# A mixture-of-experts layer whose results are scattered to token order chunk by chunk, out of a ring of eight places

## The chip, the cores and the metric

The kernel runs on one core of one Trainium2 chip. The metric is the device time of one execution in microseconds (us). All data is fp32 unless said otherwise. A core has TensorE (PE), VectorE (DVE), ScalarE (ACT), GpSimd (POOL) and SyncE (SP), which issue instructions each in its own order and meet at semaphores, and 16 DMA engines that serve the queues of SP, ACT and POOL side by side.

## What is computed

There are 2 x 1024 = 2048 tokens of 256 numbers. The first half is cross attention to 77 context rows with a residual; the second half, which holds the change, is a feed-forward layer with a shared part and 32 experts of which every token takes one:

```python
    x = x + attention(layernorm(x), ctx, ...)
    h = layernorm(x)
    shared_out = (silu(h @ shared_gate) * (h @ shared_up)) @ shared_down     # 256 -> 512 -> 256
    logits = h @ gate_w                                                      # 32 experts
    e = argmax(logits);  xs = h * sigmoid(max(logits))
    routed_out[token] = (silu(xs @ gate[e]) * (xs @ up[e])) @ down[e]        # 256 -> 512 -> 256
    out = x + shared_out + routed_out
```

## The kernel before, in words

The 2048 tokens are 16 tiles of 128 (NT = 16), handled in 8 pairs (NU = 8). Five stages follow each other.

1. Attention, second norm and gate logits of the pairs (0 to 83 us in the profile), with seven of the sixteen units of the shared part between them. One unit (`shared_up`, line 951) is 128 of the 512 inner features for 512 tokens: 8 matmuls of 512 columns on PE, a Tanh on ACT (`shared_tanh`, 745), two DVE operations (`shared_h`, 526). `shared_down` (965) is the down projection of a pair, `shared_residual` (534) adds it to x1 on DVE.
2. Routing on DVE (lines 578 to 627): the rank of each token among the tokens of its expert, the number of chunks of each expert (a chunk is up to 32 tokens of one expert, LW = 32), `slot_i`, which is 32 times a token's chunk plus its place in it, `begin`, the column in the sorted order at which each chunk starts, `chunk_end` and `turn`, tables that PE and SP read, and `block_n`, the count of groups of 16 chunks. GpSimd scatters the scaled tokens to DRAM sorted by expert, 16 indirect DMAs of 128 rows of 1 KB (line 439). Units 7 to 11 of the shared part run beside it.
3. The sorted rows are loaded back (line 353), turned on PE (1017) and copied by ACT to `xsT` (780). PE then runs unit 12 of the shared part and begins the chunks.
4. The chunk loop (130 to 256 us): 79 chunks with these inputs. For chunk c the token columns are copied from `xsT` to `x_c`, half k = 0 as soon as PE has last used it (`x0_used`) and half k = 1 after `u_done`; GpSimd does both (453 to 458), after loading the chunk's column from `begin` to a register. PE does `gate_up` (1035, matmuls at 1039), ACT takes the Silu (`silu`, 784), DVE multiplies (`gated`, 641) and turns (`turn_h`, 649), PE does `down_of` (1052, matmuls at 1061), ACT copies PSUM to SBUF (`take_y`, 789), and DVE adds the two halves of the inner features (`sum_y`, 653). PE's order is gate_up(c+1), then down_of(c). The weights of an expert are 1.5 MB. They lie in a ring of 6 places; SP fills a place again for expert e + 6 once PE has done the last chunk of expert e (`refill`, 356), so 26 experts are loaded during the loop. The results of all chunks stay in SBUF (`y_halves`, 96 chunks, in the memory named `late`). ACT stores them to `slot_rows` in DRAM in chunk order, 16 chunks in two DMAs of 256 KB (`store_y`, 794): six of these are issued in the loop, the last four after it.
5. The end: when all stores have landed (line 460), GpSimd gathers the rows of each tile by `slot_i`, 16 indirect DMAs of 128 rows (463). PE runs units 13, 14 and 15 of the shared part (1118 to 1121) and the last two down projections (1122, 1123); DVE adds the gathered rows to x1 pair by pair (682), for the last two pairs after `shared_residual`; SP writes each pair to the output (371).

What sets the order: each engine's program is written out by hand and runs in order. SP has the loads, the refills, then the outputs. GpSimd has the scatter, then the x copies, then the gathers. DVE runs `shared_h(12)`, the chunk loop, `shared_h(13..15)`, then the sums. `zeros` is written to the unused part of `slot_rows` early (344), and GpSimd clears the rest of `late` (448).

## Time and profile before

| | |
|---|---|
| median of 3 runs | 292.94 us (292.06 to 293.19) |
| the profiled execution: device time | 291.1 us |
| its span, first to last instruction | 289.2 us |
| PE busy in the span | 250.5 us (87%) |
| DVE / ACT / POOL busy | 163.1 / 94.0 / 87.9 us |
| chunks | 79 |
| chunk loop (first gate_up to the end of the last down_of) | 130.0 to 255.6 us |
| bytes moved by DMA | 68.69 MB |

The span starts at the first instruction and all times in the rows are us from there. "PEld" is PE's weight load, a name with a q at its end (SPq, POOLq) is an engine's sequencer. "idle before" and the arrow tell how long an engine stood idle and what released it; "issue" is idle time that no wait in the profile explains. Matmul records overlap, so PE's busy time is not its work at full rate. The queue q0 is GpSimd's, q1 is SP's, q10 is ACT's.

### The profile page before, as it was taken

The numbers are of one execution on the slowest core, as the hardware profiler recorded it, in microseconds if no ns is written. First come the engines' busy times: TensorE is split into PE (matmuls) and PEld (weight loads), VectorE is DVE, ScalarE is ACT, GpSimd is POOL, SyncE is SP. The second block draws the span as 40 slices with busy tenths as digits, with TensorE's granted clock in tenths as the row PEclk, the third lists the DMA queues.
The fourth block names the chain that finished last, engine by engine and source line by source line (L and its number), as shares of the span: only waits on it lengthen the run. The fifth ranks groups of instructions, "written<-read, shape, count | busy, mean of one in ns | idle before, by whom it ended". The sixth has DMA issues, their size and how long they took to land.

```text
span 289.2 us, 12925 instructions
## 1 busy us (share of the span) xinstructions
PE 250.5 (87%) x4627; PEld 184.6 (64%) x4629; DVE 163.1 (56%) x490; ACT 94.0 (33%) x284; POOL 87.9 (30%) x248
## 2 busy tenths in 40 slices
PE   4997899997799899998979999999999999698800
PEld 3765666553375358856867888788788787543700
DVE  0655796878469543016656667666666667424333
ACT  2344875454230110235323333334333333211000
POOL 1262221111005777102222223222222222103772
PEclk9996899999999999999999999999999999999985
DMA  6999994000001325401998869999999999733565
GB/s 196 328 394 410 404 401 157 2 2 1 2 0 37 109 96 165 160 16 50 329 390 286 300 236 331 358 410 415 416 410 411 415 412 409 312 83 94 174 214 164
DMA packets 32559, 68.69 MB, mean 238 GB/s; under 512 B 3966, under 2 KB 18715, under 8 KB 32539
## 3 DMA queue, kind: packets, MB, share of 16 engines
q1 hardware_dynamic: 25723, 61.60, 56.4%
q0 software_dynamic: 1536, 4.20, 4.7%
q10 hardware_dynamic: 5280, 2.62, 3.5%
q8 instruction: 13, 0.21, 0.3%
q14 instruction: 7, 0.06, 0.1%
HBM read 59.49 MB, written 8.91 MB: 237 GB/s over the span
## 4 chain that ended last, share of the span: by engine, by line
PE 66%; DMA 9%; DVE 8%; issue 5%; POOL 5%; ACT 3%; POOLq 1%; SPq 1%; ACTq 1%; DVEq 0%
PE bank L1039 23%; PE bank L961 14%; PE bank L1061 11%; DMA ring_gu<-n_L_ffn_routed_up_w_dram 5%; PE bank L973 5%; POOL xs_flat L463 5%; PE bank L874 3%; PE bank L926 2%; PE bank L909 2%; DMA slot_rows<-late 2%; DVE h_place L531 1%; ACT h_place L749 1%; DVE h_place L532 1%; DMA h_place<-in_L_xattn_kernel_q_dram 1%; DMA xs_flat<-slot_rows,slot_i 1%
## 5 line engine op out<-in xcount | busy, mean ns | idle before, releaser
L1039 PE MATMUL bank<-ring_gu,x_c 128*32 128x128 f32 x2528 | 86.8, 275 | 6.6 <-issue 2.6
L1039 PEld LDWEIGHTS bank<-ring_gu,x_c 128*32 128x32 f32 x2528 | 64.8, 109 | 20.3 <-issue 8.1
L1061 PE MATMUL bank<-ring_d,h_place 128*32 128x128 f32 x1264 | 51.8, 274 | 2.3 <-issue 1.6
L646 DVE TENSOR_TENSOR h_place<-h_place,bank 128x128 f32<-128x128 f32 x79 | 31.2, 395 | 33.2 <-PE bank L1039 30.9
L456 POOL COPY x_c<-xs_flat 128x32 f32 x79 | 16.6, 210 | 101.2 <-PE bank L1039 88.5
L1061 PEld LDWEIGHTS bank<-ring_d,h_place 128*32 128x32 f32 x1264 | 36.1, 109 | 7.7 <-DVE h_place L651 5.3
L792 ACT COPY late<-bank 128x128 f32 (+1 forms) x79 | 21.0, 266 | 57.5 <-PE bank L1061 57.5
L973 PE MATMUL bank<-shd,h_place 128*128 128x256 f32 x128 | 28.4, 380 | 2.1 <-DVE h_place L532 2.1
L651 DVE STREAM_TRANSPOSE h_place<-h_place 128x128 f32<-128x128 f32 x79 | 24.6, 311 | 9.9 <-PE bank L1061 1.7
L787 ACT ACTIVATE h_place<-bank 128x128 f32<-128x128 f32 x79 | 21.9, 277 | 23.6 <-PE bank L1039 19.3
L531 DVE SCALAR_TENSOR_TENSOR h_place<-h_place,bank 128x512 f32<-128x512 f32 x16 | 11.0, 686 | 32.5 <-ACT h_place L749 32.5
L973 PEld LDWEIGHTS bank<-shd,h_place 128*128 128x128 f32 x128 | 24.2, 190 | 6.6 <-DVE h_place L532 3.0
L961 PE MATMUL bank<-late,shg 128*128 128x512 f32 x48 | 23.1, 603 | 4.3 <-DVE h_place L532 4.2
L749 ACT ACTIVATE h_place<-bank 128x512 f32<-128x512 f32 x16 | 9.6, 597 | 51.9 <-PE bank L961 51.9
L658 DVE TENSOR_TENSOR late<-late x79 | 22.4, 283 | 3.2 <-ACT late L792 0.7
L961 PE MATMUL bank<-late,shu 128*128 128x512 f32 x48 | 22.6, 593 | 0.0
L463 POOL DMA_INDIRECT xs_flat<-slot_rows,slot_i x16 | 15.2, 950 | 16.2 <-DMA slot_rows<-late 11.7
L439 POOL DMA_INDIRECT sorted_rows<-xs_flat,pos x16 | 16.1, 1006 | 11.1 <-DVE pos L596 6.5
L458 POOL COPY x_c<-xs_flat 128x32 f32 x79 | 16.6, 210 | 1.3
L961 PEld LDWEIGHTS bank<-late,shg 128*128 128x128 f32 x48 | 8.5, 190 | 12.9 <-issue 7.2
L961 PEld LDWEIGHTS bank<-late,shu 128*128 128x128 f32 x48 | 9.1, 190 | 11.5 <-issue 11.5
L538 DVE TENSOR_TENSOR x<-bank,x 128x512 f32<-128x512 f32 x8 | 5.4, 684 | 12.2 <-PE bank L973 12.2
(132 smaller groups left out, 261.9 us busy)
## 6 DMA issues: line engine op xcount, KB each, us to landing
ring_gu<-L_ffn_routed_gate_w_dram SPq DMA_DIRECT2D x32, 512.0 KB, 9.4
ring_gu<-n_L_ffn_routed_up_w_dram SPq DMA_DIRECT2D x32, 512.0 KB, 10.3
ring_d<-L_ffn_routed_down_w_dram SPq DMA_DIRECT2D x32, 512.0 KB, 10.3
slot_rows<-late ACTq DMA_DIRECT2D x10, 256.0 KB, 6.5
x<-in_x_dram SPq DMA_DIRECT2D x4, 512.0 KB, 7.3
slot_rows<-zeros SPq DMA_DIRECT2D x1, 2048.0 KB, 20.4
late<-sorted_rows SPq DMA_DIRECT2D x8, 256.0 KB, 3.4
out_dram<-x SPq DMA_DIRECT2D x8, 256.0 KB, 2.4
```

The costliest lines, as they stand in the source:

```text
L456: g_.tensor_copy(x_c[:, 0], xsT[:, 0, bass.ds(col, LW)]).then_inc(x0_part, 1)
L458: g_.tensor_copy(x_c[:, 1], xsT[:, 1, bass.ds(col, LW)]).then_inc(x1_part, 1)
L463: g_.indirect_dma_start(out=y_t[:, i, :], out_offset=None, in_=slot_rows, in_offset=bass.IndirectOffsetOnAxis(ap=slot_i[:, i:i + 1], axis= ...
L646: v.tensor_tensor(h_r.rearrange("p (m f) -> p m f", m=KF), g_silu.rearrange(rows, m=KF), bank[1][:, 0:P].rearrange(rows, m=KF), ALU.mult). ...
L651: v.transpose(hT, h_r).then_inc(hT_ready, 1)
L658: v.tensor_tensor(sums, other, sums, ALU.add).then_inc(y_ready, 1)
L787: a_.activation(g_silu, bank[0][:, 0:P], ACT.Silu).then_inc(silu_done, 1)
L792: a_.copy(y_halves[:, bass.ds(c, 1)].rearrange("p c d -> p (c d)"), bank[2][:, 0:DH]).then_inc(y_taken, 1)
L961: ins = te.matmul(dst[:], w[:, k, m * P:(m + 1) * P], xnT_of(g)[:, k], start=(k == 0), stop=(k == KD - 1))
L973: ins = te.matmul(bank[4 + w % 2][:, j * D:(j + 1) * D], h_s[:, w // 2 % 2, m, c:c + P], shd[:, m], start=(m == 0), stop=(m == KF - 1))
L1039: ins = te.matmul(bank[g][q * LW:(q + 1) * LW, 0:P], x_c[:, k], ring_gu[:, s, g, k, q * P:(q + 1) * P], start=(k == 0), stop=(k == KD - 1))
L1061: ins = te.matmul(bank[2][r:r + LW, 0:DH], hT[:, f * LW:(f + 1) * LW], ring_d[:, s, f, a * DH:(a + 1) * DH], start=(m == 0), stop=(m == HA ...
```

## The change

Each chunk's result now goes to DRAM by itself, in token order, in rows of half a token (512 B): GpSimd issues one indirect DMA of 64 rows for each chunk (rounded up to groups of eight chunks: 80 scatters for 79 chunks) to the table `y_rows`. Padding rows go to spare rows behind the table. The results lie in a ring of eight places, `y_ring`. `take_y` waits for its place to be free (`y_free`); GpSimd frees the place of chunk k - 2 (LAG = 2) after it has issued the scatter of chunk k and waited for that of k - 2 to land. After the last has landed, SP loads the table in order, 8 plain DMAs of 256 KB (1 KB rows, contiguous for a token), and then issues the outputs.

GpSimd no longer copies token columns: ACT does, between `silu` and `take_y`, after loading the chunk's column to a register. ACT's stores, the zeros, GpSimd's clear of `late` and the 16 gathers are gone. The row numbers are new work: four small functions on DVE between units 7 to 10 of the shared part make one-hot tables in bf16, PE multiplies them (16 matmuls of 64 weight columns and 104 columns, before unit 12), and DVE turns the product into row numbers. `groups_n` (three DVE instructions) takes the place of `block_n` (two). At the end DVE adds the loaded rows for all eight pairs first and the last two shared residuals after that; SP waits for both.

```diff
 GpSimd
-            with pool.Fori(0, n_chunks) as c:
-                col = pool.value_load(begin[0:1, bass.ds(c, 1)], min_val=0, max_val=T)
-                pool.wait_ge(x0_used, c + FREE1)
-                g_.tensor_copy(x_c[:, 0], xsT[:, 0, bass.ds(col, LW)]).then_inc(x0_part, 1)
-                pool.wait_ge(u_done, c + FREE1)
-                g_.tensor_copy(x_c[:, 1], xsT[:, 1, bass.ds(col, LW)]).then_inc(x1_part, 1)
-            pool.wait_ge(y_stored, HALVES * 16 * (blocks + 1))
-            pool.sem_inc(pool_waited, 1)
-            for i in range(NT):
-                g_.indirect_dma_start(
-                    out=y_t[:, i, :], out_offset=None, in_=slot_rows,
-                    in_offset=bass.IndirectOffsetOnAxis(ap=slot_i[:, i:i + 1], axis=0)).then_inc(y_in[i // 2], 16)
+            def next_rows(c, k):
+                g_.tensor_copy(rows_now[:, k:k + HALF_RING], rows_all[:, bass.ds(c, HALF_RING)]).then_inc(row_copied, 1)
+            def store_group(b, first=False):
+                for k in range(Y_RING):
+                    pool.wait_ge(row_copied, 2 * b + 1 + k // HALF_RING)
+                    pool.wait_ge(y_ready, Y_RING * b + k + 1)
+                    pool.sem_inc(y_sent, 1)
+                    g_.indirect_dma_start(
+                        out=y_rows, out_offset=bass.IndirectOffsetOnAxis(ap=rows_now[:, k:k + 1], axis=0),
+                        in_=y_ring[0:HR, k, :], in_offset=None).then_inc(y_out[k], 16)
+                    gone = (k - LAG) % Y_RING
+                    if k >= LAG:
+                        pool.wait_ge(y_out[gone], 16 * b + 16)
+                        pool.sem_inc(y_free, 1)
...
+                    if k == LAG:
+                        next_rows(Y_RING * b + HALF_RING, HALF_RING)
+                    if k == LAG + HALF_RING:
+                        next_rows(Y_RING * b + Y_RING, 0)
+            next_rows(0, 0)
+            store_group(0, first=True)
+            with pool.Fori(1, groups) as b:
+                store_group(b)
+            for k in range(Y_RING - LAG, Y_RING):
+                pool.wait_ge(y_out[k], 16 * groups)
+            pool.sem_inc(y_landed, 1)
 SyncE, behind the refills
+            sp.wait_ge(y_landed, 1)
+            for u in range(NU):
+                sp.dma_start(y_t[:, 2 * u:2 * u + 2], y_by_token[:, 2 * u:2 * u + 2]).then_inc(y_in[u], 16)
             for u in range(NU):
                 sp.wait_ge(sum_ready, u + 1)
+                if u >= NU - 2:
+                    sp.wait_ge(residual_ready, u + 1)
                 sp.dma_start(out_t[:, 2 * u:2 * u + 2], x1[:, 2 * u:2 * u + 2]).then_inc(out_done, 16)
 ScalarE
-            def take_y(c):
+            def take_y(c, place_c):
                 act.wait_ge(down_done, c + 1)
-                a_.copy(y_halves[:, bass.ds(c, 1)].rearrange("p c d -> p (c d)"), bank[2][:, 0:DH]).then_inc(y_taken, 1)
+                act.wait_ge(y_free, c + 1)
+                a_.copy(y_ring[:, place_c].rearrange("p c d -> p (c d)"), bank[2][:, 0:DH]).then_inc(y_taken, 1)
+            def take_x(c, col):
+                act.wait_ge(x0_used, c + FREE1)
+                a_.copy(x_c[:, 0], xsT[:, 0, bass.ds(col, LW)]).then_inc(x0_part, 1)
+                act.wait_ge(u_done, c + FREE1)
+                a_.copy(x_c[:, 1], xsT[:, 1, bass.ds(col, LW)]).then_inc(x1_part, 1)
+            def chunk(c):
+                col = column(c + 1)
+                silu(c)
+                take_x(c + 1, col)
...
             shared_tanh(3 * KF)
+            act.wait_ge(begin_ready, 1)
+            act.wait_ge(xsT_ready, NU + 1)
+            take_x(0, 0)
+            chunk(0)
+            with act.Fori(0, groups) as b:
+                for k in range(Y_RING):
+                    chunk(Y_RING * b + k + 1)
+                    take_y(Y_RING * b + k, slice(k, k + 1))
 VectorE, the end
+            for u in range(NU):
+                dve.wait_ge(y_in[u], 16)
+                rows = x1[:, 2 * u:2 * u + 2]
+                v.tensor_tensor(rows, rows, y_t[:, 2 * u:2 * u + 2], ALU.add).then_inc(sum_ready, 1)
+            for u in range(NU - 2, NU):
+                dve.wait_ge(sum_ready, NU)
+                shared_residual(u)
 TensorE, before unit 12 of the shared part
+            pe.wait_ge(hot_ready, 3)
+            for i in range(NT):
+                ins = te.matmul(bank[3][0:2 * LW, 0:SLOTS], hot_t[:, i].rearrange("p a t -> p (a t)"), hot_c[:, i],
+                                start=(i == 0), stop=(i == NT - 1))
+            ins.then_inc(found_done, 1)
```

## Rows read from the trace of the kernel before

**Rows 1.** Busy time by stretch (core 0: us, busy and count by engine, PEclk, DMA share, GB/s)

```profile
190.00:252.00 62.00, 58.48 (x1920) 49.59 (x1913) 39.44 (x120) 21.72 (x80) 16.36 (x79) 1.00 1.02 407
252.00:289.20 37.20, 20.35 (x140) 12.38 (x131) 13.38 (x24) 2.87 (x7) 15.62 (x18) 0.88 0.50 142
```

**Rows 2.** The chain of work that ended last (start us, us, what)

```profile
235.93 15.02 DMA ring_gu<-n_L_ffn_routed_up_w_dram
...
258.14 5.12 DMA slot_rows<-late
...
282.98 2.82 DMA xs_flat<-slot_rows,slot_i
```

**Rows 3.** The page's costliest groups: the gathers (busy us, mean ns, idle before)

```profile
L463 POOL DMA_INDIRECT xs_flat<-slot_rows,slot_i x16 | 15.2, 950 | 16.2 <-DMA slot_rows<-late 11.7
```

**Rows 4.** Timeline after the chunk loop (start us, us, engine line op, idle before)

```profile
255.55 1.99 PE L961 MATMUL bank<-xnT_last,shg 128*128 128x512 f32 x4
...
267.50 0.69 DVE L532 SCALAR_TENSOR_TENSOR h_place<-h_place,bank 128x512 f32<-128x512 f32 x1
...
268.24 7.17 PE L973 MATMUL bank<-shd,h_place 128*128 128x256 f32 x32 [2.13 <-DVE h_place L532]
...
285.90 0.69 DVE L682 TENSOR_TENSOR x<-x,xs_flat 128x512 f32<-128x512 f32 x1 [1.06 <-DMA xs_flat<-slot_rows,slot_i]
```

**Rows 5.** DMA issues by line (KB each, median us from issue to landing)

```profile
late<-sorted_rows SPq DMA_DIRECT2D x8, 256.0 KB, 3.4
```

**Rows 6.** GpSimd's scatter of stage 2, line 439, and one piece of its timeline

```profile
L439 POOL DMA_INDIRECT sorted_rows<-xs_flat,pos x16: 956/960/1437, 89.7 to 109.4; - x16
DMA to landing us min/median/max: 2.4/2.4/3.2
91.17 1.44 POOL L439 DMA_INDIRECT sorted_rows<-xs_flat,pos  x1 [0.30 <-issue]
```

**Rows 7.** Timeline of the chunk loop, one chunk

```profile
201.47 0.21 POOL L458 COPY x_c<-xs_flat 128x32 f32 x1
...
201.56 1.08 PE L1039 MATMUL bank<-ring_gu,x_c 128*32 128x128 f32 x32
201.86 0.27 ACT L792 COPY late<-bank 128x128 f32 x1 [0.68 <-PE bank L1061]
...
202.26 0.28 ACT L787 ACTIVATE h_place<-bank 128x128 f32<-128x128 f32 x1
202.35 0.28 DVE L658 TENSOR_TENSOR late<-late  x1
```

**Rows 8.** A table load to a register on PE's sequencer, line 1069

```profile
L1069 PEldq TENSOR_LOAD <-turn x32: 283/288/317, 130.3 to 251.3; - x32
```

**Rows 9.** Groups of instructions of ACT, shapes apart: the smallest copy-like one

```profile
L729 ACT ACTIVATE half_tanh<-top 128x2 f32<-128x2 f32 x8 | 1.5, 191 | 0.0
```

**Rows 10.** Timeline of the routing on DVE

```profile
93.78 0.14 DVE L624 TENSOR_SCALAR block_n<-block_n 1x1 int32<-1x1 int32 x1
```

**Rows 11.** The chain again: sixteen small matmuls in stage 1

```profile
53.19 0.69 PE bank L909 x16
```

**Rows 12.** Timeline at the start of the chunk loop

```profile
130.10 0.60 ACT L749 ACTIVATE h_place<-bank 128x512 f32<-128x512 f32 x1 [2.85 <-PE bank L961]
...
130.74 1.28 ACT L787 ACT_TABLE_LOAD   x1
...
132.04 0.28 ACT L787 ACTIVATE h_place<-bank 128x128 f32<-128x128 f32 x1
```

**Rows 13.** DMA queues and issues from 190 to 250 us (packets, MB, share of 16 engines)

```profile
q10 hardware_dynamic: 2112, 1.05, 5.8%
...
slot_rows<-late ACTq DMA_DIRECT2D x3, 256.0 KB, 9.5
```

**Rows 14.** DMA queues from 88 to 112 us, the scatter of stage 2

```profile
q0 software_dynamic: 768, 2.10, 24.4%
```

**Rows 15.** Waits from 140 to 255 us: PE's weight loads behind the x copies

```profile
PEld bank L1039 <- POOL x_c L456: 3.1, 8, 0.7
```

More of the change, by code:

```diff
@@ L289, in build_cross_attention_moe @@
         FREE2 = 2
+        LAG = 2
+        HALF_RING = Y_RING // 2
         EARLY_PARTS = {t: t - 7 for t in range(7, NU + 6)}
@@ new lines, in next_rows @@
+            def next_rows(c, k):
[12 more added lines that the diff above has]
+                        pool.sem_inc(y_free, 1)
+                    elif not first:
+                        pool.wait_ge(y_out[gone], 16 * b)
+                        pool.sem_inc(y_free, 1)
+                    if k == LAG:
+                        next_rows(Y_RING * b + HALF_RING, HALF_RING)
+                    if k == LAG + HALF_RING:
+                        next_rows(Y_RING * b + Y_RING, 0)
@@ new lines, in column @@
+            def column(c):
+                return nc.values_load(begin[0:1, bass.ds(c, 1)], engines=(mybir.EngineType.Activation,), min_val=0, max_val=T,
+                                      skip_runtime_bounds_check_because="held to the number of tokens where it is written")
+            def take_x(c, col):
[3 more added lines that the diff above has]
+                a_.copy(x_c[:, 1], xsT[:, 1, bass.ds(col, LW)]).then_inc(x1_part, 1)
@@ L826, in _ @@
+            with act.Fori(Y_RING * groups + 1, n_chunks) as c:
+                chunk(c)
+                take_y(c - 1, place_of(c - 1))
+            take_y(n_chunks - 1, place_of(n_chunks - 1))
             for n in range(3 * KF + 1, 4 * KF):
@@ L831, in _ @@
             te = nc.tensor
+            pe.sem_inc(y_free, Y_RING)
             for credit in (y_taken, y_taken, silu_done, h_ready, hT_ready, x0_used, u_done):
```

139 lines of the change are left out of this document (77 added, 62 removed).

## The prediction

> **What bounds the kernel now.** I read the busy time by stretch first. From 190 to 252 us PE is busy 58.5 of 62 us at full clock, and the DMA engines are full as well (share 1.02, 407 GB/s); ACT's 80 instructions are two for each chunk, so 40 chunks take 62 us, 1.55 us each. From 252 us on the picture is another one: PE is busy 20 of 37 us, DMA half, POOL 15.6 us [rows 1]. The chain of waits says what rules there. Up to 251 us it is PE's chunks and, last, 15.0 us of a weight load, so the end of the loop hangs on PE and on the DMA queues together. Then come 5.1 us for the last store and POOL's gathers, the last of them starting at 281.73, with 2.8 us more until it has landed [rows 2]. The group of the gathers has sixteen of 0.95 us, and each is followed by an idle 0.3 us (4.6 of the 16.2 us idle before the group, the other 11.7 being the wait for the stores): 1.25 us for each 128 rows, 20 us in all [rows 3]. The timeline of the end shows PE and DVE working beside this: unit 13 starts at 255.55, the last `shared_h` ends at 268.19, the last down projections run 268.24 to 275.41, and the last sum ends at 286.59, 2.6 us before the span's end [rows 4]. So 11 us lie between the end of the shared part and the last sum, and only the gathers fill them.
>
> **Part by part.** The profiled execution took 291.1 us with a span of 289.2; the median of the runs is 292.9, 1.8 above it. I reckon in the span and add the difference to both.
>
> *The end.* Stores, gathers and their wait go. What is late next? The scatter of the last chunk starts at about 256.6 (take and sum are 0.27 and 0.28 us [rows 7]). With the spare one behind it, 1.26 us later, and 2.4 us to land [rows 6] the table is complete at 260.3. SP then issues eight loads of 256 KB; the same form took 3.4 us to land [rows 5], and 2.1 MB at 407 GB/s [rows 1] are 5.2 us, so all are in by 269. DVE is free at 268.2, and eight sums of 0.69 us end at 273.7, `shared_residual(6)` at 274.4. The last `shared_residual` must wait for PE until 275.4 anyway. It ends at 276.2 (0.69 and waits), and with the same 2.6 us behind it the span ends at **278.8, a gain of 10.4 us** [rows 4]. The table path has 1.0 us to spare. PE's 19.8 us of shared work behind the loop are now the bound.
>
> *Ahead of the loop.* `groups_n` costs one more small DVE step, 0.16 us (0.14 and its wait [rows 10]), and PE waited for DVE there: +0.16. The four table functions are 0.9 to 2.2 us each between units that PE paces at 3.4 us and in which DVE works 1.4, so they are hidden (without that cover they would cost 5 us). The 16 new matmuls stand in PE's path: sixteen of 64 weight columns and 77 columns took 0.69 us [rows 11], times 104/77 is +0.9; the bounds are 0.7 and 1.5. Their DVE work, 1.6 us, lies under unit 12. At the loop's start ACT now copies x behind the Tanh. Before, the Tanh ended at 130.70, the table of Silu was loaded meanwhile, and the first Silu ran at 132.04, when PE had long been done [rows 12]. Now Tanh, one copy of 0.19 (the nearest row has 2 columns and 191 ns; 32 columns add little [rows 9]), 0.7 us until the gate matmuls are done (201.56 to 202.26 [rows 7]), and only behind that wait the 1.28 us table load: Silu at 133.0, +0.96. If the load is made ahead of the wait it is +0.4. Sum: **+2.0** (1.3 to 2.6).
>
> *ACT in the loop.* Per chunk: Silu 0.28, take 0.27, two copies of 0.19 and a column load to a register, 0.29 us on the sequencer [rows 7, 8, 9]: 1.22 us against the fastest period of 1.4 and the mean of 1.55. The column load runs under take_y and would let Silu start at 202.2 where it started at 202.26. The copy of the second half follows `u_done` as POOL's did; POOL's ended at 201.68, and PE, starting at 201.56, needs it 0.2 us later [rows 7]. It is close but not late. Bounds: a gain of 3.1 us (PE's waits behind POOL's copies [rows 15]) and a loss of 0.1 us per chunk, 7.9. I take **+1.0**, near the row of the unhindered chunk.
>
> *DMA in the loop.* The writes are the same 2.6 MB in 512 B rows, but the part after the loop (four of ten stores) moves into it, where the queues are full from 190 us on. There 2112 packets of ACT's queue took 5.8% of 16 engines for 60 us, 26 ns each [rows 13]. The 39 chunks of that stretch are 2496 rows: 384 more, 0.6 us. In GpSimd's own queue 2048 rows of 1 KB took 24.4% of 24 us, 46 ns each [rows 14]; by that it is 7.2 against 3.5 us, +3.7. I take **+0.6**, since rows of the same size are nearer. It delays the last weight load and all behind it.
>
> *GpSimd in the loop.* 0.96 and 0.30 us for a scatter [rows 6], under 0.1 for row numbers, and two waits and two increments more: about 1.4 us per chunk, under 1.55. Three scatters are in flight (LAG 2), so a landing of up to 3 x 1.4 = 4.2 us is free. Idle it takes 2.4 us [rows 6]. Under load a store of 32 rows per DMA engine took 9.5 us [rows 13], so (9.5 - 2.4)/32 = 0.22 per row, and four rows make 3.3. Cost 0; the ring covers short lags. The cleared memory and zeros lay under idle time: 0.
>
> Sum: 278.8 + 2.0 + 1.0 + 0.6 = 282.4 for the span, 6.8 less; from the median **286.2 us**.
>
> **The rivals.**
> *A. GpSimd's pace rules (slower).* If no place of the ring is free, ACT waits for `y_free` ahead of take_y; the next Silu and x copies are queued behind it, and PE and DVE wait for those. The second scatter of stage 2 ran while DVE was working without a pause and took 1.44 us plus 0.30, not 1.26 [rows 6]; in the loop DVE works two thirds of the time. At 1.75 us the 80 scatters are 140 us against 125.6: +14.4 in place of +1.0, a span of 295.8, 299.5 by the median. It decides from (125.6 + 7.8)/80 = 1.67 us per scatter, or a landing of 5.0. Against it: only two of sixteen rows were long, and a copy of POOL in the loop took its usual 0.21 us beside DVE [rows 7]. The Trainium skill (SBUF — State Buffer, "SBUF: two separate sides") says that a GpSimd operation fully blocks while a DVE operation in a 2-port mode, or one with two SBUF inputs, holds the shared ports. By that rule a scatter would wait up to 0.28 us for each `sum_y`, 1.4 + 0.28 = 1.68: just at the deciding point. The long scatter agrees; nothing in the loop of before can show it. Chance 0.17.
> *B. ACT's chain rules.* x_c comes 0.1 us late in every chunk: +7.9 for +1.0, span 289.3, no change (293.1). For it: 1.22 of 1.4 us are taken with no semaphore delay counted. Chance 0.12, a third of it slower.
> *C. The ring is full at the loop's end.* Eight scatters of 1.26 are left: landed at 269, loads in at 275.7, sums and residuals to 277.8, span 280.4 + 3.6 = 284.0, 287.8 by the median. Still faster. Chance 0.08.
> *D. The small scatters hold the DMA engines.* At 46 ns a row, span 285.5 (289.3). Chance 0.05. The Trainium skill (DMA: Bandwidth & Descriptors, "Measured (HBM→SBUF, 128 partitions, SWDGE, issued from GpSimd)") gives 0.68 us for 4 KB and 0.95 for 64 KB; if these held all engines, 39 scatters would be an estimated 31 us. The scatter of 128 rows took 0.37 us of the engines [rows 14], so I give that nothing.
>
> **How the numbers follow.** Forecast 0.58, A 0.17, B 0.12, C 0.08, D 0.05. A measurement here can tell about 0.5%, 1.5 us. Faster than that: forecast, C, D, less what lies at the edge, 0.70; the same 0.09 (B, mostly); slower 0.21 (A and the rest of B). The range: the low end takes the start at 1.3, DMA at 0 and a gain of 1 us in pace, 282.8; the high end holds B, C and D, 294.5; A stays out.
>
> **What would show it.** Right: the group of gathers gone; the last shared_down about 20 us behind the loop's end, and the last `shared_residual` waiting for it; POOL's scatters in pace with the chunks, landing in 3 to 4 us; the first Silu near 135; 1.55 us per chunk. Wrong: take_y's idle time ending on POOL or on a scatter's landing (A); PE or its weight loads waiting for ACT's copies of x_c (B); DVE's sums waiting for the table after 276 (C); longer weight loads with PE behind them (D).

## The result, and the profile after

The changed kernel took 307.11 us (median of 4 runs, 304.97 to 308.51) against 293.06 us of the kernel before on the same chip: ratio 1.0498, interval [1.045, 1.0546]. The forecast was 286.2 us, with 294.5 as the upper end of its range. It is slower where I forecast faster. The profiled execution took 306.29 us with a span of 304.4.

Here is the page of the changed kernel: its busy time, the shares of its ending chain, and its costliest groups.

```profile
span 304.4 us, 13052 instructions
...
PE 259.0 (85%) x4643; PEld 185.2 (61%) x4645; DVE 169.1 (56%) x505; ACT 121.0 (40%) x445; POOL 112.0 (37%) x173
...
PE 48%; DMA 27%; DVE 9%; issue 9%; ACT 3%; POOL 2%; POOLq 1%; SPq 1%; ACTq 0%; DVEq 0%
...
L474 POOL DMA_INDIRECT y_rows<-y_ring,rows_now x80 | 72.7, 909 | 74.2 <-DMA y_rows<-y_ring,rows_now 29.1
...
L1148 PE MATMUL bank<-ring_d,h_place 128*32 128x128 f32 x1264 | 51.0, 275 | 17.7 <-ACT y_ring L868 16.8
...
L868 ACT COPY y_ring<-bank 128x128 f32<-128x128 f32 (+1 forms) x79 | 21.0, 265 | 46.4 <-POOLq L480 26.3
```

DMA was 27% of the chain (of before, one long weight load and a few short pieces [rows 2]), and POOL waited 29.1 us for scatters to land. ACT stood idle 46.4 us before `take_y`, most of it until POOL released a place of the ring. The waits say the same, chained from scatter to ACT to PE (us in total, times, longest):

```profile
POOL y_rows L474 <- DMA y_rows<-y_ring,rows_now: 29.1, 20, 3.9
ACT y_ring L868 <- POOLq L480: 26.3, 19, 2.7
PE bank L1148 <- ACT y_ring L868: 16.8, 19, 1.8
ACT y_ring L868 <- POOLq L483: 10.3, 11, 1.9
```

Busy time by stretch in the loop (as in [rows 1]):

```profile
180.00:200.00 20.00, 15.78 (x480) 12.31 (x480) 9.89 (x30) 8.68 (x41) 9.53 (x12) 1.00 0.81 310
200.00:220.00 20.00, 15.70 (x476) 12.35 (x480) 9.62 (x30) 8.22 (x40) 9.40 (x13) 1.00 1.03 412
220.00:240.00 20.00, 17.98 (x591) 14.62 (x580) 12.11 (x37) 10.79 (x48) 11.84 (x16) 1.00 0.77 259
240.00:260.00 20.00, 14.47 (x443) 11.09 (x432) 8.85 (x28) 7.70 (x36) 8.57 (x11) 1.00 1.03 414
```

A chunk is 48 matmuls: 476 and 443 in 20 us are 2.0 and 2.2 us for each chunk where the DMA engines are full (share 1.03), 591 are 1.6 where they are less so (0.77); before it was 1.55 with full engines [rows 1]. The rule is rough: the first stretch has 480 at a share of 0.81, and from 270 to 279 us 224 matmuls at a share of 0.11 are still 1.93 us for each chunk. The chain shows what a landing costs, piece by piece (start us, us, what):

```profile
198.24 5.50 DMA y_rows<-y_ring,rows_now
...
203.87 5.11 DMA y_rows<-y_ring,rows_now
...
210.00 5.14 DMA y_rows<-y_ring,rows_now
...
216.09 4.97 DMA y_rows<-y_ring,rows_now
```

The timeline brackets the loop: its first matmuls, the copies and table load ahead of the first Silu, the last `down_of`, the last `shared_down`, and the last `shared_residual` behind it:

```profile
132.69 0.21 ACT L877 COPY x_c<-xs_flat 128x32 f32<-128x32 f32 x1
...
133.00 1.08 PE L1126 MATMUL bank<-ring_gu,x_c 128*32 128x128 f32 x32 [0.84 <-issue]
133.03 1.28 ACT L862 ACT_TABLE_LOAD   x1
...
134.33 0.28 ACT L862 ACTIVATE h_place<-bank 128x128 f32<-128x128 f32 x1
...
278.62 0.64 PE L1148 MATMUL bank<-ring_d,h_place 128*32 128x128 f32 x16 [0.68 <-ACT y_ring L868]
...
291.89 8.86 PE L1055 MATMUL bank<-shd,h_place 128*128 128x256 f32 x32 [2.13 <-DVE h_place L562]
...
300.86 0.69 DVE L568 TENSOR_TENSOR x<-bank,x 128x512 f32<-128x512 f32 x1 [0.95 <-PE bank L1055]
```

From these rows I use one measure for every kernel below. **Loop** is from the start of the first gate_up to that of the last down_of; **tail** is from there to the end of the span. Each is one profiled execution.

| kernel | start | loop | tail | span |
|---|---|---|---|---|
| before | 130.0 | 125.0 | 34.2 | 289.2 |
| changed | 133.0 | 145.6 | 25.8 | 304.4 |

The tail gave 8.4 us back, the start took 3.0, the loop took 20.6.

### The profile page after: what moved, and what is told of

It reads as the page before. It is cut to its first block, busy times and chain, and to the rows that moved or that the text cites. A ratio compares the mean times of both kernels' runs of the same rounds, so it can differ in the third digit from the quotient of the medians.

```text
span 304.4 us, 13052 instructions
## 1 busy us (share of the span) xinstructions
PE 259.0 (85%) x4643; PEld 185.2 (61%) x4645; DVE 169.1 (56%) x505; ACT 121.0 (40%) x445; POOL 112.0 (37%) x173
## 4 chain that ended last, share of the span: by engine, by line
PE 48%; DMA 27%; DVE 9%; issue 9%; ACT 3%; POOL 2%; POOLq 1%; SPq 1%; ACTq 0%; DVEq 0%
DMA y_rows<-y_ring,rows_now 25%; PE bank L1043 17%; PE bank L1126 8%; PE bank L1055 7%; PE bank L1148 4%; PE bank L956 3%; PE bank L1008 2%; PE bank L991 2%; DVE h_place L561 2%; DVE h_place L562 1%; POOL y_rows L474 1%; DMA bq_row<-in_L_xattn_bias_q_dram 1%; ACT h_place L824 1%; PE bank L939 1%; PE bank L1000 1%
## 5 line engine op out<-in xcount | busy, mean ns | idle before, releaser
L474 POOL DMA_INDIRECT y_rows<-y_ring,rows_now x80 | 72.7, 909 | 74.2 <-DMA y_rows<-y_ring,rows_now 29.1
L1148 PE MATMUL bank<-ring_d,h_place 128*32 128x128 f32 x1264 | 51.0, 275 | 17.7 <-ACT y_ring L868 16.8
L1148 PEld LDWEIGHTS bank<-ring_d,h_place 128*32 128x32 f32 x1264 | 33.9, 109 | 28.1 <-issue 23.3
L868 ACT COPY y_ring<-bank 128x128 f32<-128x128 f32 (+1 forms) x79 | 21.0, 265 | 46.4 <-POOLq L480 26.3
L1055 PE MATMUL bank<-shd,h_place 128*128 128x256 f32 x128 | 30.1, 396 | 2.1 <-DVE h_place L562 2.1
L1055 PEld LDWEIGHTS bank<-shd,h_place 128*128 128x128 f32 x128 | 25.4, 200 | 7.1 <-DVE h_place L562 3.0
L1043 PE MATMUL bank<-late,shg 128*128 128x512 f32 x48 | 24.1, 626 | 5.0 <-DVE h_place L562 4.9
L730 DVE TENSOR_TENSOR y_ring<-y_ring x79 | 22.6, 286 | 3.6 <-ACT y_ring L868 1.0
L453 POOL DMA_INDIRECT sorted_rows<-xs_flat,pos x16 | 16.4, 1023 | 11.0 <-DVE pos L626 6.4
L877 ACT COPY x_c<-xs_flat 128x32 f32 (+1 forms) x80 | 17.2, 216 | 3.1 <-PE bank L1126 2.2
L879 ACT COPY x_c<-xs_flat 128x32 f32 (+1 forms) x80 | 17.3, 216 | 1.1
L434 POOL TENSOR_SCALAR var<-mv 128x2 f32<-128x2 f32 x8 | 1.8, 221 | 30.9 <-DVE mv L515 30.9
```

The lines of the kernel that those rows point to most:

```text
L474: g_.indirect_dma_start(out=y_rows, out_offset=bass.IndirectOffsetOnAxis(ap=rows_now[:, k:k + 1], axis=0), in_=y_ring[0:HR, k, :], in_offs ...
L730: v.tensor_tensor(sums, other, sums, ALU.add).then_inc(y_ready, 1)
L868: a_.copy(y_ring[:, place_c].rearrange("p c d -> p (c d)"), bank[2][:, 0:DH]).then_inc(y_taken, 1)
L877: a_.copy(x_c[:, 0], xsT[:, 0, bass.ds(col, LW)]).then_inc(x0_part, 1)
L879: a_.copy(x_c[:, 1], xsT[:, 1, bass.ds(col, LW)]).then_inc(x1_part, 1)
L1043: ins = te.matmul(dst[:], w[:, k, m * P:(m + 1) * P], xnT_of(g)[:, k], start=(k == 0), stop=(k == KD - 1))
```

## The experiments

All spans below are to be read with the scatter of such executions in mind: the kernel before itself ran from 289.94 to 297.64 us in 23 runs beside the last four experiments, and a few profiles (`no_scatter`, `split_stores_16`) have a spell near 150 to 165 us in which the granted clock was 0.89 and PE did 330 to 350 matmuls in 15 us, not 475. A difference of 4 us between single spans is not a finding; `light_loads`, `lag1` and all kernels from `no_scatter` to `scatters_in_bursts` below were run once. The experiments came in five lots, each on another chip (`after_third`, `no_scatter`, `half_scatters` and `before_plus_scatters` are one lot); where a ratio is given it is to the kernel before of the same lot. `lag3`, `ring16_lag6`, `light_loads` and `before_act_x` are one lot, `after_again` and `lag1` another.

**More landings in flight.** If only the landing of `y_rows` held the loop, more scatters in flight would cure it.

```diff
-        LAG = 2
+        LAG = 3
```


> The changed kernel with LAG = 3 in place of 2: GpSimd has four scatters in flight instead of three before it waits for a landing. Theory L (latency): a scatter lands about 6 us behind its start while the weight loads keep the queues full, whatever else is in flight, so the chunk period in the full stretches was 6/3 = 2.0 us and becomes 6/4 = 1.5 us, which is PE's own period. The loop shrinks from 146 us to about 130, the span from 304 to about 288. Theory R (rate): the DMA engines serve GpSimd's queue only at one scatter per 2 us beside the weight loads, so one more in flight only lengthens the landing to 8 us: loop 146, span 304. Theory A (ScalarE's chain with the copies of the token columns is the bound): also 304.

```diff
-    Y_RING = 8
+    Y_RING = 16
-        LAG = 2
+        LAG = 6
```


> The changed kernel with a ring of 16 places and LAG = 6: seven scatters in flight. Theory L: 6/7 is under 1 us per chunk, so no wait of ScalarE for a place is left, the loop is PE's and the weight loads': 127 to 130 us, start at 133, tail 24, span 284 to 287. Theory R: nothing gained, 300 or more. Theory A: ScalarE's waits for PE and the copies stay, loop 140 or more, span above 296.

**The weight loads taken away.** The refills bring 16 of 128 partitions, so the weights are mostly old ones.

```diff
-                load_gate_up(e + RING, s)
+                few = slice(0, 16)
+                sp.dma_start(ring_gu[few, s, 0], ex_gate_w[bass.ds(e + RING, 1)].rearrange("a (p k) f -> p (a k) f", p=P)[few]).then_inc(gu_in[s], 16)
...
```


> The changed kernel whose 26 refills load 16 of 128 partitions of each weight, an eighth of the bytes, with the same number of loads and semaphores (so 26 experts compute with stale weights; the loads are all that is left out). Theory L with the load as its cause: a scatter lands in 2.2 to 2.5 us, three in flight allow 0.8 us per chunk, GpSimd's 1.25 us are no bound, no wait for a place is left, loop 115 to 122 us, span 272 to 280. If the latency belongs to the small scatter itself and not to the load, the landing stays at 6 us, the loop at 146, the span at 304.

Measured: `lag3` 355.56 us, ratio 1.2134 [1.2046, 1.2223]; `ring16_lag6` 355.7 us, ratio 1.2192 [1.2079, 1.2305]; `light_loads` 353.99 us in one run. All three are near 355, none is what any theory said. Either the edits cost 50 us each, or something was different in this lot. So the changed kernel itself had to be run again.

> The changed kernel once more, unedited, as a control beside the next two. Its first run took 307 us and stood on the places it waited to be free; lag3, ring16_lag6 and light_loads, which have little in common, all took 354 to 356 us with other waits (signals of TensorE that ScalarE and VectorE get 1 to 3 us late). Theory V (the edits don't matter; an execution of any kernel with the scatters in the loop falls into one of two modes by chip or by place in memory): 355 here. Theory E (each edit does it, by letting GpSimd run further ahead): 305 to 308 here.

> LAG = 1, two scatters in flight. Theory L (a landing takes 6 us under load): 3.0 us per chunk in the full stretches, loop above 190 us, span 350 or more with ScalarE waiting for places in the ring for tens of us. Theory E, by which a GpSimd that is held back more disturbs less: the late signals are absent and the loss is all waits for places. If the time isn't set by landings: 305.

Measured, on another chip: the unedited changed kernel 352.07 us, ratio 1.2025 [1.1918, 1.2133]; LAG = 1 356.16 us (one run). A third control (`after_third`) gave this on one more chip:

> The changed kernel unedited, in the same job as control: it took 305 to 308 us in its first four runs and 349 to 353 in the second four. Theory V (a mode by chip or load of the program): one of the two again, 350 more likely, since five other kernels with the scatters were in it.

351.75 us, ratio 1.1942 [1.1887, 1.1998]. **So the changed kernel has two levels of time:** 307 us in its first four runs, near 352 us in all six later ones, on both chips that these used, while the kernel before stayed at 291 to 295. Against the control, LAG 1, 3 and 6, the larger ring and the light loads are all within 2%, three of them across chips: at the upper level neither the lag, the ring nor the weight loads make the difference. The loop lengths say it too: 192.1 and 189.2 us for the controls, 196.1, 196.0, 196.1 and 195.4 for the four edits.

The trace of `after_third` shows another picture than the first one. ACT's wait for a ring place is no longer among its larger waits; what is new is idle time of PE inside its own run of matmuls. Here are the groups of PE and of its weight loads:

```profile
L1148 PE MATMUL bank<-ring_d,h_place 128*32 128x128 f32 x1264 | 70.9, 279 | 15.0 <-issue 11.1
L1148 PEld LDWEIGHTS bank<-ring_d,h_place 128*32 128x32 f32 x1264 | 42.0, 111 | 31.9 <-issue 25.5
```

The other engines wait too, and for something that the profile can't name ("remote"). In its wait table, DVE before `gated`:

```profile
DVE h_place L717 <- remote: 39.8, 16, 2.6
```

In the loop of each of the eight traces of the upper level whose scatters are one per chunk, such waits come to 34 to 76 us on ACT and 37 to 62 us on DVE; in the first trace of the changed kernel and in the kernel before they come to less than 2 us.

**ScalarE's copies alone.** The kernel before with the x copies and the column load on ACT.

```diff
 GpSimd
-                g_.tensor_copy(x_c[:, 0], xsT[:, 0, bass.ds(col, LW)]).then_inc(x0_part, 1)
...
 ACT, between silu and take_y
+                a_.copy(x_c[:, 0], xsT[:, 0, bass.ds(col, LW)]).then_inc(x0_part, 1)
+                act.wait_ge(u_done, c + FREE1)
+                a_.copy(x_c[:, 1], xsT[:, 1, bass.ds(col, LW)]).then_inc(x1_part, 1)
```


> The kernel before with one part of the change alone: ScalarE, not GpSimd, loads the column and copies the token columns, in the order of the changed kernel; stores, gathers and the rest as before. The prediction's size: +1.0 us at the loop's start (the table load of Silu behind the copies) and +1.0 in the loop, span 291. Theory A: the copies on ScalarE cost 0.1 us or more per chunk, loop 8 us longer, span 297 or more. If ScalarE's copies come earlier than GpSimd's did: 289 or less.

Measured: 295.29 us over 10 runs, ratio 1.0083 [1.0045, 1.012]; start 131.3, loop 126.7, tail 34.3. In the single profile the start costs 1.3 and the loop 1.7 us, and the ratio of the runs, 2.4 us, is of that size. ACT's copies are not what slows the change.

**The scatters taken out.** The changed kernel where a semaphore increment stands for each of the 80 scatters, and the end loads `sorted_rows` in place of the table (the routed results are left out of the output).

```diff
-                    g_.indirect_dma_start(
-                        out=y_rows, out_offset=bass.IndirectOffsetOnAxis(ap=rows_now[:, k:k + 1], axis=0),
-                        in_=y_ring[0:HR, k, :], in_offset=None).then_inc(y_out[k], 16)
+                    pool.sem_inc(y_out[k], 16)
```


> The changed kernel without the 80 scatters of the loop: GpSimd waits and signals as before, with an increment where each scatter stood; the load at the end reads the sorted rows in place of the table (left out: storing the routed results, so the sums take other rows). Theory S (the scatters themselves slow TensorE and the signals): the loop is PE's and the weight loads' again, 124 to 130 us, span 279 to 285. Theory A (ScalarE's copies or the new order of its program are the cause of the long waits): 340 or more, as in the last six runs.

Measured: 286.64 us, span 284.8 (start 134.4, loop 124.8, tail 25.6), in one run, beside 294.56 of the kernel before. Everything but the scatters is about as forecast, whose span was 282.4; `after_third`, of the same lot, is 64.7 us longer, 0.81 us for each scatter.

**The same with every other scatter.** Results of odd chunks are left out of the table.

```diff
+                    if k % 2:
+                        pool.sem_inc(y_out[k], 16)
+                    else:
...
```


> The changed kernel with a scatter for every even chunk alone (left out: storing the odd ones; the load at the end reads the sorted rows). Theory S with a price per scatter: half way between no_scatter and the full kernel, about 315 if these are 280 and 350. If the price hangs on the pace (scatters closer than some 1.5 us disturb and others don't): under 295.

Measured: span 303.8, loop 147.5 against 124.8 of `no_scatter`: +22.7 for 40 scatters, 0.57 each, where 80 cost the loop 64.4, 0.81 each (`after_third`). This kernel shows best what one scatter does, since every second chunk has none. Below are one gate_up, the scatter beside it and the Silu of that chunk; first the changed kernel in its first trace, then `half_scatters`:

```profile
229.77 1.10 PE L1126 MATMUL bank<-ring_gu,x_c 128*32 128x128 f32 x32
230.23 0.92 POOL L474 DMA_INDIRECT y_rows<-y_ring,rows_now  x1 [0.17 <-issue]
230.48 0.28 ACT L862 ACTIVATE h_place<-bank 128x128 f32<-128x128 f32 x1 [0.21 <-PE bank L1126]
```
```profile
221.44 1.08 PE L1129 MATMUL bank<-ring_gu,x_c 128*32 128x128 f32 x32
221.86 0.92 POOL L477 DMA_INDIRECT y_rows<-y_ring,rows_now  x1 [1.87 <-DVE y_ring L733]
223.22 0.28 ACT L865 ACTIVATE h_place<-bank 128x128 f32<-128x128 f32 x1 [1.38 <-PE bank L1129]
```

The scatter starts at nearly the same place of the chunk (0.46 and 0.42 us behind gate_up's start), but the Silu comes 0.71 us behind it in the first and 1.78 in the second. In the timeline of `half_scatters` from 140 us on, counted over the gate_ups that it shows in one piece, all 33 Silus with a scatter beside their gate_up come over 0.9 us behind its start (median 1.77), and all 20 without one come at 0.70. At the upper level every scatter does it: 39 of 39 in `after_third`, 33 of 33 in the next kernel. In the first trace of the changed kernel the median of 57 such Silus is 0.76, and 25 are over 0.9.

**Scatters that nobody waits for.** The kernel `before_act_x` with 72 needless ones behind `y_ready`, at most three in flight; neither ACT nor PE depends on them.

```diff
+                    pool.wait_ge(y_ready, 8 * b + k + 1)
+                    pool.sem_inc(d_sent, 1)
+                    g_.indirect_dma_start(
+                        out=spare_rows, out_offset=bass.IndirectOffsetOnAxis(ap=pos[0:HR, k:k + 1], axis=0),
+                        in_=zeros[0:HR, 0, 0:DH], in_offset=None).then_inc(d_out[k], 16)
...
```


> before_act_x (span 292) with work added that nobody waits for: beside the chunk loop GpSimd issues 72 scatters of 64 rows of 512 B from a constant tile into a table that isn't read, one per chunk, at most three in flight, as the changed kernel does. No ring, no y_free. Theory S: each scatter costs the core some 0.6 us whatever waits on it, so the span rises by 72 x 0.6 = 43 to about 335. Theory L (only the wait of ScalarE for a free place costs, and nobody waits here): 292 to 296.

Measured: span 355.5, loop 186.5 against 126.7 for the same kernel without them. With no ring and no release to wait for, the loop still grew by 60 us. So at the upper level it isn't the ring: the scatter beside the loop slows TensorE and what waits for it. Its timeline, first PE, then POOL, then ACT:

```profile
207.92 0.49 PE L1095 MATMUL bank<-ring_d,h_place 128*32 128x128 f32 x9
208.60 0.33 PE L1095 MATMUL bank<-ring_d,h_place 128*32 128x128 f32 x2 [0.20 <-issue]
209.39 0.32 PE L1095 MATMUL bank<-ring_d,h_place 128*32 128x128 f32 x2 [0.46 <-issue]
210.14 0.42 PE L1095 MATMUL bank<-ring_d,h_place 128*32 128x128 f32 x3 [0.43 <-issue]
210.66 1.08 PE L1073 MATMUL bank<-ring_gu,x_c 128*32 128x128 f32 x32
```
```profile
202.26 0.90 POOL L460 DMA_INDIRECT spare_rows<-zeros,pos  x1 [2.77 <-DVE late L673]
203.68 0.90 POOL L460 DMA_INDIRECT spare_rows<-zeros,pos  x1 [0.52 <-issue]
207.29 0.90 POOL L460 DMA_INDIRECT spare_rows<-zeros,pos  x1 [2.72 <-DVE late L673]
208.73 0.90 POOL L460 DMA_INDIRECT spare_rows<-zeros,pos  x1 [0.55 <-issue]
```
```profile
210.17 0.28 ACT L802 ACTIVATE h_place<-bank 128x128 f32<-128x128 f32 x1 [2.67 <-remote]
```

The reader is to see sixteen matmuls that have all their operands: nine run in 0.49 us, the other seven need from 208.41 to 210.56. They come two or three at a time, with gaps that end on no wait. The Silu at 210.17 waits for gate matmuls of a group that PE started at 207.00 and, by the records, had behind it when it began the next one at 207.92: the signal reached ACT over 2 us late. The scatters fall in pairs 1.4 us apart, every 5.0 us for two chunks. Beside the pair before, PE stood 1.51 us for a copy of ACT's that had itself waited 1.30 us on "remote".

**What in a scatter does it?** Four kernels of one lot, all from `before_plus_scatters`, with the one instruction exchanged (each added line stands in place of the scatter).

```diff
 scatters_16_rows
-                        out=spare_rows, out_offset=bass.IndirectOffsetOnAxis(ap=pos[0:HR, k:k + 1], axis=0),
+                        out=spare_rows, out_offset=bass.IndirectOffsetOnAxis(ap=pos[0:16, k:k + 1], axis=0),
...
 plain_gpsimd_dmas
+                    g_.dma_start(spare_rows[HR * k:HR * (k + 1)], zeros[0:HR, 0, 0:DH]).then_inc(d_out[k], 16)
 act_small_stores (in take_y, none on GpSimd)
+                act.dma_start(spare_c[:, bass.ds(c, 1)], zeros[0:HR, :, 0:DH]).then_inc(d_out[0], 16)
 gpsimd_compute
+                    g_.tensor_tensor(out=busy_tile[:, 3 * k:3 * k + 3], in0=ones_scan[:, 0:3], in1=power[:, 0:3], op=ALU.pow).then_inc(d_out[k], 16)
```


> The kernel before_plus_scatters with its 72 unneeded scatters cut from 64 rows to 16 rows of 512 B each. Theory 1 (a fixed price for each DMA that GpSimd makes, about 0.85 us of the loop, whatever its size): span again 345 to 357 us, GpSimd busy 0.7 to 0.9 us on each. Theory 2 (price by row, as 64 descriptors and rows would have it): a quarter of the 63 us over the kernel without scatters (292.3), so a span near 308.

> The same 72 places, each with a plain DMA issued by GpSimd (64 rows of 512 B to one stretch, no indices). Theory 1 (what stops TensorE is a DMA of GpSimd whatever its kind): span 345 to 357. Theory 2 (it is the indirect one alone, its indices or its work on GpSimd): span 292 to 297.

> No GpSimd DMA in the loop; ScalarE issues one plain store of the same 64 rows of 512 B behind each of its 79 copies out of PSUM. Theory 1 (small DMAs in flight of any kind slow the instructions' supply or TensorE): span 340 or more. Theory 2 (only those that GpSimd makes): 292.3 plus at most 79 issues of 0.1 us on ScalarE, so 292 to 300.

> The same 72 places on GpSimd with the same waits and semaphore counts, but a power of 128x3 elements (near 0.9 us of GpSimd's time by the 128x2 and 128x4 rows) instead of a DMA. Theory 1 (the DMA is what costs): span 292 to 294. Theory 2 (a busy GpSimd or its semaphores in the loop cost): span 340 or more.

| kernel | instruction on GpSimd | loop | tail | span |
|---|---|---|---|---|
| `before_act_x` | none | 126.7 | 34.3 | 292.3 |
| `gpsimd_compute` | 850 ns of power | 127.9 | 34.5 | 295.1 |
| `plain_gpsimd_dmas` | 534 ns, DMA_DIRECT2D | 130.8 | 38.0 | 299.8 |
| `act_small_stores` | none | 139.3 | 35.3 | 305.6 |
| `scatters_16_rows` | 840 ns, DMA_INDIRECT | 181.0 | 37.8 | 348.1 |
| `before_plus_scatters` | 897 ns, DMA_INDIRECT | 186.5 | 37.7 | 355.5 |

```profile
L460 POOL DMA_INDIRECT spare_rows<-zeros,pos x72 | 60.4, 840 | 127.5 <-DVE late L673 78.7 <-issue 28.2 <-DMA spare_rows<-zeros,pos 20.5
```
```profile
L460 POOL DMA_DIRECT2D spare_rows<-zeros x72 | 38.4, 534 | 108.1 <-DVE late L671 57.1 <-DMA spare_rows<-zeros 45.3 <-issue 4.5
```

(First the scatters of 16 rows, then the plain DMAs; the first and the last kernel of the table ran on two other chips than the four between.) A quarter of the rows costs the loop 54.3 us in place of 59.8, so the price is nearly all by the DMA, not by the row. A GpSimd that is as busy but makes no DMA costs about 1 us, plain DMAs of GpSimd 4 us. The stores on ACT cost the loop 12.6 us, but on ACT: 18% of that kernel's chain is ACT's own sequencer (3% in `before_act_x`), which issues them between Silu and copies, and PE's group L1079 stood idle 2.0 us in all. Of these four only the indirect scatters stop PE.

**Gathers, and scatters in bursts.** Again from `before_plus_scatters`; the gathers have 64 rows of 256 B.

```diff
 gathers_in_loop
+                        out=idle_rows[0:HR, k % 4, :], out_offset=None, in_=sorted_quarters,
+                        in_offset=bass.IndirectOffsetOnAxis(ap=pos[0:HR, k:k + 1], axis=0)).then_inc(d_out[k], 16)
 scatters_in_bursts
+                pool.wait_ge(y_ready, 8 * b + 8)
                 for k in range(8):
-                    pool.wait_ge(y_ready, 8 * b + k + 1)
```


> The kernel before_plus_scatters, but the 72 unneeded DMAs are indirect gathers (64 rows of 256 B from memory to a spare tile), not scatters. Theory 1 (an indirect DMA of GpSimd stops TensorE, whichever way it goes): span 345 to 357. Theory 2 (it is the scattered writing): 292 to 300, as with the plain DMAs.

> The kernel before_plus_scatters, with its 72 unneeded scatters in nine bursts of eight, each behind the eighth chunk, not one behind each chunk. Theory 1 (each scatter stops TensorE by itself, some 0.85 us): again 345 to 357. Theory 2 (a stop is a pair's, or an overlap with a fixed place in the chunk): fewer stops, 300 to 330.

Measured: gathers loop 132.7, tail 42.8, span 305.3; bursts loop 134.0, tail 47.6, span 312.6. The long tails are a backlog: the last needless DMAs started at 273.33 and 280.88, behind the loops' ends, and the real gathers stood behind them. The loops grew by 6 and 7 us only. Of the bursts, 58 scatters fell between 140 and 262 us. So in this run the same scatters, as dense, left the loop almost alone. **That their order or the gathers' direction is the reason is not shown,** since no control ran on this chip. A stretch of each, the kernel with a scatter per chunk and the one with bursts:

```profile
220.00:225.00 5.00, 3.83 (x107) 2.59 (x101) 1.97 (x6) 1.98 (x9) 1.84 (x2) 1.00 1.04 407
225.00:230.00 5.00, 3.89 (x93) 2.52 (x94) 1.96 (x6) 1.48 (x7) 2.23 (x3) 1.00 0.86 312
```
```profile
220.00:225.00 5.00, 5.00 (x172) 4.41 (x176) 3.51 (x11) 3.06 (x13) 2.16 (x3) 1.00 1.04 409
225.00:230.00 5.00, 4.95 (x168) 3.89 (x164) 3.34 (x12) 3.19 (x15) 2.32 (x3) 1.00 1.04 411
```

POOL is as busy (1.84 and 2.23 against 2.16 and 2.32 us), the DMA engines are as full, the granted clock is 1.00 in both, and PE does 100 matmuls against 170. In PE's timeline of the loop from 140 us on I counted the gaps over 0.3 us: 18 in the first trace of the changed kernel, 48 in `after_third`, 45 in `before_plus_scatters`, but 9 with bursts and 9 with gathers. That count can't decide, for `half_scatters`, where every scatter delays its chunk, has only 7. The last two ran on a chip on which no kernel with a scatter per chunk was run, so this comparison crosses chips; on each of the four chips of the other lots such kernels were at the upper level. By the delay of the Silu (medians of 0.81 with bursts and 0.80 with gathers beside gate_up) these two look like the first trace of the changed kernel (0.76), so the lower level is a rival that stands.

**A way to have part of the gain.** If the end of the kernel before hangs on four stores in a row (3.41 us of ACT's sequencer) and a landing, the stores can be shared between two queues and made smaller, with no scatter in the loop.

```diff
 ACT, behind the loop
-            act.wait_ge(y_ready, STORE * blocks)
-            for a in range(HALVES):
-                store_y(blocks - 1, a)
             act.wait_ge(y_ready, n_chunks)
-            for a in range(HALVES):
-                store_y(blocks, a)
+            store_y(blocks, 1)
 SP, behind the refills
+            sp.wait_ge(y_ready, STORE * blocks)
+            for a in range(HALVES):
+                store_y_sp(blocks - 1, a)
+            sp.wait_ge(y_ready, n_chunks)
+            store_y_sp(blocks, 0)
```


> The kernel before, with the last but one block's two stores moved from ScalarE's end to SyncE (which issues them as soon as that block is summed) and the last block's two stores shared between the two queues; scatters only in stage 2 as before. If the tail of before hangs on its stores (four issues of ScalarE, 3.41 us in a row, then a landing of 5 us, then 16 gathers), the gathers start about 2 us sooner than 264.15 and the end goes from 289.2 to about 287.1 of span, ratio 0.993. If the landing hangs on the DMA queues' load alone, no change: ratio 1.000.

> The same with blocks of 8 chunks in place of 16: the last stores carry half the bytes. Landing of the last ones 3.5 to 4.5 us in place of 5; the end about 286 of span, ratio 0.990, unless the ten more issues on ScalarE cost the loop something (each at most 0.85 us of ScalarE, which waits for TensorE there): then 289 or more.

Measured: 16 chunks in a block, 293.16 us, ratio 1.0003 [0.9958, 1.0049]; 8 chunks, 291.75 us, ratio 0.9959 [0.991, 1.0007]. The tails are 32.9 and 31.0 us against 34.2, so the second did get its 3.2 us there. Here is its group of gathers, which starts 5.4 us behind the last down_of (259.39), where the one of before started 9.2 us behind (254.97 and 264.15):

```profile
L477 POOL DMA_INDIRECT xs_flat<-slot_rows,slot_i x16: 942/946/1371, 264.8 to 284.1; - x16
```

In the times 0.4% is seen, and the interval still holds no change. The version with 16 chunks was profiled in an execution of 295.08 us, 2 us above its median, so its tail says little. It is the best of the versions that compute the whole output, and not shown to beat the kernel before.

## Why the prediction was wrong

**The end: right in mechanism, 2 us too large.** The gathers are gone; the tail is 8.4 us shorter, in place of 10.4. As said, the last `shared_residual` waits for PE and not for the table. The difference is nearly all one term: the last down projections took 8.86 us where I had taken 7.17 from before [rows 4]. The granted clock was 0.81 over them and 1.00 over those of before; in `light_loads`, `ring16_lag6` and `half_scatters`, whose last three slices all have 0.9 or more, the tail is 23.8 to 23.9 us. The table was later than forecast: the last scatter started 8.0 us behind the last `down_of` (286.63), not 2.9, and DVE's last sum ended at 299.19. It would have been the bound, as in rival C, had PE not been late as well; that part was luck. (Rival C's own sum is 2 us short: from a table complete at 269 the loads, 8.7 us in the forecast, are in by 277.7, not 275.7.)

**Ahead of the loop: +3.0, forecast +2.0.** The 16 matmuls took 0.92 us as reckoned from [rows 11]. Tanh, copies, table load came in the order I gave, and the first Silu ran at 134.33. What was missed: PE had to wait 0.84 us for the first x copy, which on ACT can only come behind the Tanh of unit 12; I had counted only the Silu's delay. `before_act_x` has this alone and starts 1.3 us late.

**ACT in the loop: +1.0 taken, +1.7 measured** (`before_act_x`), inside the bounds. Rival B is refuted as the cause of the loss.

**DMA in the loop: +0.6, not measured by itself.** `no_scatter` can't separate it, since the writes are part of the scatters. `plain_gpsimd_dmas`, with 72 writes of the same rows more, has a loop 4.1 us longer; that is about the scatter of single spans, and far from 20. Rival D is not the cause either.

**GpSimd in the loop: the step that failed.** "Cost 0" rested on two things. The pace of the instruction was right: 80 scatters, and their own durations move little, although DVE works beside them:

```profile
L474 POOL DMA_INDIRECT y_rows<-y_ring,rows_now x80: 891/897/1024, 139.3 to 286.6; - x80
```

So the part of rival A that drew on the long scatter of stage 2 doesn't carry the time. The Trainium skill (SBUF — State Buffer, "SBUF: two separate sides") would have added up to 0.28 us to scatters that meet `sum_y`. This trace agrees in kind, not in weight. Here is the longest of the 80:

```profile
184.09 0.28 DVE L730 TENSOR_TENSOR y_ring<-y_ring  x1
184.15 1.02 POOL L474 DMA_INDIRECT y_rows<-y_ring,rows_now  x1 [0.16 <-issue]
```

The seven scatters that started with 0.16 to 0.22 us of a running `sum_y` left took 0.96 to 1.02 us, all others at most 0.94; together that is 0.7 us. The long one of stage 2 (1.44 us [rows 6]) fits: it started with 0.60 us left of a DVE product of two inputs in SBUF (91.08 to 91.77 us in the profile of before). The other way round nothing was held back: 37 `sum_y` that began inside a scatter took their usual 0.28 us.

The other thing was the landing, "(9.5 - 2.4)/32 = 0.22 per row, and four rows make 3.3". Measured in the first trace are 5.0 to 5.5 us in the chain behind an issue of 0.9, so about 6 us from the start where the queues are full. I had scaled the wait by rows, as if a short DMA waited in proportion for its own rows. With three in flight 6 us make 2.0 us for each chunk, which is the pace of the stretches with a DMA share of 1.03. That is rival A's second condition, "a landing of 5.0", and it was met. Its time, 299.5 us, was worked out for the first condition, scatters 1.75 us apart, so that it lies near the 307 is luck: 2.0 us for each of 80 would be 160 us of loop if the queues were full throughout, and the loop took 145.6. Rival A had a chance of 0.17; the landing, not the pace of GpSimd, was what deserved the weight. In the first trace ACT waited 36.6 us for places of the ring, and PE 16.8 us for ACT behind that, of the 20.6 us lost. That is read from waits and not shown by an experiment, since the runs that were to test it (`lag3`, `ring16_lag6`, `light_loads`) fell on the upper level. Nor is it all: from 262 to 279 us ACT waited less than 3 us for places, and the loop was still slower than 1.55 us for each chunk.

**And one effect that no case held.** In all later runs with a scatter per chunk the loop was slowed beside the scatters, by 0.8 us for each: PE got its matmuls out late and ACT and DVE got its signals late. No step of the forecast has a term for GpSimd's DMAs acting on TensorE. Shown are these points, each by one run and most by 50 us: it is caused by the scatters (`no_scatter`), not by any wait for them (`before_plus_scatters`), hardly by their rows (`scatters_16_rows`), not by GpSimd's work or semaphores (`gpsimd_compute`), and plain DMAs of the same bytes hardly do it (`plain_gpsimd_dmas`). I could have known that nothing in the profile of before bounds this: its indirect DMAs stand beside matmuls of 512 columns, or of 256 in the tail, a few instructions per microsecond; the loop has 31 matmuls and as many weight loads in one.

**Open** are three things. Why the first four runs were at 307 us and all later ones near 352, whereas the kernel before didn't move. What the stop is: a shortage of instructions at PE would look as these gaps do, but no view shows PE's supply, I did not test it, and it would not explain a Silu that waits 2 us for matmuls that PE has behind it. And whether bursts or gathers escape it: their one run each may simply have been at the lower level. That bursts drift against the chunk, while a scatter per chunk meets the same place of PE's program each time, is only argued, and the pair of stretches under `half_scatters` speaks against it: at the same place of the chunk one level has the delay and the other has not. The changed kernel with its own scatters in bursts was not tried.

## What to carry to other kernels

An indirect DMA from GpSimd is not free because its engine is idle: measure one in the loop where it is to stand, beside the instructions it is to stand beside, before building on it. A stand-in that nobody waits for (72 needless scatters) and its absence (an increment in place of it) separate "waited for" from "in the way" in two runs. When a small DMA goes into full queues, its landing is not its own rows' share of a long one: 64 rows of 512 B took about 6 us, where 128 rows of 1 KB had taken 2.4 in stage 2 [rows 6]. By that as many must be in flight as the loaded landing is periods long, an estimate of four here (6 over 1.55), not three; no run at the lower level tested it. And repeat the control in each lot: without it, three edits here would have been blamed for 50 us that they didn't cost, and in the last lot, which had none, the bursts and gathers can't be judged.

## What the runs showed of the hardware

- At the upper level, indirect scatters issued once per chunk cost the loop 0.8 us each (59.8 us for 72), while a plain DMA of GpSimd cost less than a tenth of it (4.1 us for 72). Matmuls with all operands present came two or three at a time for about 2 us, and a Silu beside a scatter came a median of 1.74 to 1.83 us behind gate_up's start in place of 0.70.
- The cost is nearly all by the DMA: 16 rows 181.0 us of loop, 64 rows 186.5.
- A scatter of 64 rows that starts under a running DVE sum of two inputs in SBUF, with 0.16 to 0.22 us of it left, takes 0.96 to 1.02 us in place of 0.90; one of 128 rows with 0.60 us left took 1.44 in place of 0.96.
- The sixteen scatters of 128 rows in stage 2 took 1.0 us each (1006 ns before, 1023 after), and in neither of these traces has PE a gap beside them that ends on no wait.
- One kernel can have two levels of time that differ by 15% with the kernel before unmoved in between (291 to 295 us).
- A small store of 32 KB issued by ACT once a chunk made the loop 12.6 us longer over 79 chunks, 0.16 us each (one run).
